# Routed experts of a gated Mamba/MoE layer: all tokens through all eight experts, against 40 sorted blocks of 256 chosen pairs

## The reference

```python
# branch s: Mamba block, 256 inner channels, 64 states
dt = softplus(x_ssm @ dt_w + dt_b)
state = state * exp(dt_t * A) + (dt_t * x_t)[:, :, None] * B_t[:, None, :]    # 512 steps, per channel and state
y_t   = einsum('bds,bs->bd', state, C_t)
s     = xn + ((y + x_ssm * D) * silu(z)) @ Wout
# branch g: 2 shared experts on every token, 8 routed experts of which the 2 best count
h_s    = experts(rmsnorm(xn), W1_s, b1_s, W2_s, b2_s).sum(experts)
scores = sigmoid(xn @ centroids)
gpk, i_topk = top_k(scores, 2);  gk = gpk / scores.sum(-1)
routed_all  = experts(rmsnorm(xn), W1_r, b1_r, W2_r, b2_r)        # 128 -> 512 -> gelu -> 128, dense in the reference
h_r    = (gk * take_along_axis(routed_all, i_topk)).sum(chosen)
g      = xn + h_s + h_r
```

## Time and profile before

| | us |
|---|---|
| median of 3 runs (lowest, highest) | 1951.54 (1948.29, 1955.75) |
| the profiled execution's own time | 1950.72 |
| its span, first to last instruction | 1949.0 |
| busy over the span: PE, DVE, ACT, POOL | 1700.5, 1851.6, 1344.5, 1333.7 |
| mean granted TensorE clock | 0.973 |

### The profile page before, as it was taken

One profiled execution on the slowest core, in us unless ns is written; L12 is line 12 of the kernel. 1 busy time (PEld: TensorE's weight loads), 2 busy tenths in 40 slices (PEclk: granted clock), 3 DMA queues, 4 the chain that ended last, 5 costly groups with the idle time before them and its releaser, 6 DMA issues.

```text
span 1949.0 us, 41413 instructions
## 1 busy us (share of the span) xinstructions
PE 1700.5 (87%) x10512; PEld 677.8 (35%) x10512; DVE 1851.6 (95%) x2100; ACT 1344.5 (69%) x2196; POOL 1333.7 (68%) x604
## 2 busy tenths in 40 slices
PE   1667579999999999999999999999999999999997
PEld 1433233333333333333333333333333333333332
DVE  6799669999999999999999999999999999999997
ACT  1478657777677777776777767777777677776773
POOL 6020057777777767776777777776777677777776
PEclk9689789999999999999999999999999999999999
DMA  4334455556555645564554745574566555465543
GB/s 126 119 111 148 148 152 118 116 117 153 123 116 121 163 118 122 120 146 130 118 117 116 162 121 115 122 161 119 122 119 148 133 120 115 117 161 120 116 116 93
DMA packets 191302, 248.49 MB, mean 127 GB/s; under 512 B 18714, under 2 KB 95140, under 8 KB 191084
## 3 DMA queue, kind: packets, MB, share of 16 engines
q1 hardware_dynamic: 191252, 247.76, 52.8%
HBM read 221.76 MB, written 25.30 MB: 127 GB/s over the span
## 4 chain that ended last, share of the span: by engine, by line
issue 32%; PE 27%; DVE 20%; POOL 10%; ACT 5%; SPq 2%; DVEq 2%; DMA 1%; ACTq 1%; POOLq 0%
DVE arena L910 10%; POOL arena L525 7%; DVE ps L900 6%; PE ps L1088 6%; PE ps L1074 6%; PE ps L1128 4%; PE ps L1120 4%; POOL arena L520 3%; ACT arena L676 1%; PE ps L1060 1%; PE ps L983 1%; PE ps L1134 1%; DMA gate_scratch<-arena 1%; SPq L250 1%; PE ps L1037 1%
## 5 line engine op out<-in xcount | busy, mean ns | idle before, releaser
L525 POOL TENSOR_TENSOR arena<-arena 128x1024 f32<-128x1024 f32 x512 | 1206.6, 2366 | 540.7 <-DVE arena L910 383.6
L910 DVE TENSOR_TENSOR_SCAN arena<-arena,ps 128x512 f32<-128x512 f32 x1024 | 1184.3, 1213 | 13.1 <-PE ps L1074 7.7
L676 ACT ACTIVATE arena<-arena,neg_A 128x512 f32 (+1 forms) x1024 | 657.9, 711 | 96.9 <-DVE arena L910 96.0
L1088 PE MATMUL ps<-arena,ident 64*64 64x512 f32 x4096 | 556.6, 615 | 3.2 <-POOL arena L525 3.2
L900 DVE TENSOR_TENSOR ps<-arena,ps 128x512 f32<-128x512 f32 x768 | 495.0, 697 | 17.9 <-PE ps L1060 16.9
L1120 PE MATMUL ps<-x_rms,arena 128*128 (+1 forms) x640 | 345.0, 637 | 74.6 <-ACT arena L698 72.1
L698 ACT ACTIVATE arena<-ps,b1r_sb 128x512 f32<-128x512 f32 x256 | 169.0, 686 | 270.8 <-PE ps L1120 270.0
L1074 PE MATMUL ps<-arena 128*64 128x128 f32 x4096 | 282.0, 280 | 23.5 <-DVE arena L910 18.1
L1074 PEld LDWEIGHTS ps<-arena 128*64 128x64 f32 x4096 | 220.5, 137 | 234.8 <-DVE arena L910 119.7
L1128 PE MATMUL ps<-arena 128*128 128x512 f32 x512 | 264.4, 618 | 0.0
L1120 PEld LDWEIGHTS ps<-x_rms,arena 128*128 128x128 f32 x640 | 101.6, 189 | 273.4 <-ACT arena L698 159.8
(11 more groups left out here) (122 smaller groups left out, 781.2 us busy)
## 6 DMA issues: line engine op xcount, KB each, us to landing
arena<-c_scratch SPq DMA_DIRECT2D x128, 1024.0 KB, 8.6
arena<-w_routed_scaled SPq DMA_DIRECT2D x128, 128.0 KB, 4.2
arena<-in_L_ffn_W_r_dram SPq DMA_DIRECT2D x64, 256.0 KB, 4.1
arena<-gate_scratch SPq DMA_DIRECT2D x64, 256.0 KB, 3.6
arena<-w_shared_tiles SPq DMA_DIRECT2D x128, 64.0 KB, 1.8
arena<-dt_scratch SPq DMA_DIRECT2D x9, 512.0 KB, 9.3
arena<-u_scratch SPq DMA_DIRECT2D x9, 512.0 KB, 10.2
arena<-xs_scratch SPq DMA_DIRECT2D x18, 256.0 KB
```

What stands on the lines that cost most here:

```text
L525: nc.gpsimd.tensor_tensor(products[:, i % RING, :, :], states[:, i % 2, :, :], c_rows[:, i // CG, i % CG, :].unsqueeze(1).broadcast_to((P, ...
L676: nc.scalar.activation(decay[:, 2 * i + h, :], dflat[:, ds(slot + h * L, L)], ACT.Exp, scale=aflat[:, ds(col, 1)]).then_inc(s["decay_ready ...
L910: vector.tensor_tensor_scan(states[:, i % 2, h, :], decay[:, m, :], ps[bank][:], 0.0, ALU.mult, ALU.add).then_inc(s["scanned"], 1)
L1088: ins = mm(y_ps[r][HP * h:HP * h + HP, :], ident[q, q], products[q, slot, h, :], start=False, stop=False, skip_group_check=True)
```

## The change

The routed experts no longer run on all tokens. In the preamble DVE picks the two best experts per token (`choose_experts`), PE counts by two matmuls how many pairs come before each token, and DVE gives each pair a row in a list sorted by expert, each expert rounded up to 256 rows (`place_tokens`). POOL scatters each token's normalised row to its two places by 64 indirect DMAs of 128 rows into a table that SP has filled with zeros. The sorted list has 40 blocks of 256 rows. Groups 0 to 39 (batches 0 to 4) take one block each, SP reading the block's expert from SBUF. Groups 40 to 63 take none. There POOL gathers the routed rows back by 64 indirect DMAs, three a group, and PE adds them, gated by diagonal matrices, into the final sum of each batch (`add_rows`). Per batch, the sums of both branches go through DRAM (`ffn_d`, `attn_d`), and the last steps of a batch (silu, product, turn, copy) come in three of the groups from 42 on. `KIND` becomes `DEDEDEDE`. W1 is scaled on ACT. `turns` is a Python list now, so that the preamble and the last three batches are written out and not looped.

```diff
-    KIND = "DDEDDDED"
+    KIND = "DEDEDEDE"
+    GATHERS = TOPK * TPB
+    GATHER_AT = (1, 4, 7)
...
+            sp.wait_ge(s["constants_made"], N_MASK)
+            sp.dma_start(x_sorted_d.rearrange("(n p) c -> p n c", p=P),
+                         zeros.unsqueeze(1).broadcast_to((P, NBLK * BK, C))).then_inc(s["zeros_stored"], 16)
...
-                load_w2(b, g)
-                load_gate(b, g)
-                load_w2_shared(b, g)
+                if block:
+                    load_w2(u, e)
+                if block_before:
+                    store_routed(u - 1)
+                load_w2_shared(u, g)
...
-            pool.wait_ge(s["w1_staged"], 32)
-            for g_col, a, n in ((g_routed_col, 0, E), (g_shared_col, E, ES)):
-                nc.gpsimd.tensor_scalar(w1_stage[:, a * H:(a + n) * H], w1_stage[:, a * H:(a + n) * H], g_col, None,
-                                        ALU.mult).then_inc(s["w1_scaled"], 1)
...
+            for j in range(NT):
+                for k in range(TOPK):
+                    nc.gpsimd.indirect_dma_start(x_sorted_d, bass.IndirectOffsetOnAxis(slots[:, k, j:j + 1], 0),
+                                                 rms_tok[:, j, :], None).then_inc(s["x_sorted"], 16)
+            pool.wait_ge(s["x_sorted"], 16 * TOPK * NT)
...
+            def gather(q):
...
+                nc.gpsimd.indirect_dma_start(rows[:, f % 2, at, :], None, routed_d,
+                                             bass.IndirectOffsetOnAxis(slots[:, k, f * TPB + j:f * TPB + j + 1], 0)
+                                             ).then_inc(s[f"rows_gathered{f % 2}"], 16)
...
+            def evict_block(m):
+                act.wait_ge(s["block_made"], m + 2)
+                act.wait_ge(s["routed_stored"], m * 16 + 16)
+                nc.scalar.copy(routed_out, block_ps[:, RA].rearrange("p (n c) -> p n c", c=C)
+                               ).then_inc(s["block_evicted"], 1)
...
+            def evict_attn(b):
+                act.wait_ge(s["attn_projected"], b + 2)
+                act.wait_ge(s["attn_stored"], b * 16 + 16)
+                nc.scalar.copy(attn_out, ffn_ps[:]).then_inc(s["attn_evicted"], 1)
...
+                    for t in range(HT):
+                        act.wait_ge(s["tile_made"], u * HT + (HT + t // 2 * 2 + 2))
+                        src = block_ps[:, (RA, RB)[t]] if t < 2 else hid_ps[:, (RA, RB)[t - 2]]
+                        nc.scalar.activation(hidden_block[:, t, :], src, ACT.Gelu, bias=b1_block[:, t:t + 1]
+                                             ).then_inc(s["tile_gelu"], 1)
...
+                    if i == 4 and block_before:
+                        evict_block(u - 1)
+                    if i == 6 and block:
+                        copy_x_block(u)
...
+                hidden_tiles(u, g, block)
+                if head and last is not None:
+                    evict_attn(last)
...
+                if k == 0:
+                    dve.wait_ge(s["w1_scaled_stored"], 32)
+                vector.tensor_tensor(rms_tok[:, j, :], xn_tok[:, j, :], bc3(stats[:, 7, j], C), ALU.mult
                                     ).then_inc(s["rms_made"], 1)
...
+            choose_experts()
+            for b, odd in turns:
                 convolve(b, b * NL + (base + NCONV - NL))
+                if b == 2:
+                    place_tokens()
...
-                    if i == SG - 2:
-
-                        dve.wait_ge(s["gate_row_loaded"], b * (16 * E) + g * 16 + 16)
-                        dve.wait_ge(s["expert_added"], b * E + g + 1)
-                        dve.wait_ge(s["expert_made"], b * E + g + 1)
-                        vector.tensor_tensor(gated_expert, expert_ps[:], gate_row, ALU.mult
-                                            ).then_inc(s["expert_gated"], 1)
+                    if last is not None and i == 2:
+                        gate_y(last)
...
+            def turn_x(m):
+                pe.wait_ge(s["x_rows_loaded"], m * 16 + 16)
+                pe.wait_ge(s["block_evicted"], m + 1)
+                for k in range(BK):
+                    ins = nc.tensor.transpose(block_ps[:, k * P:(k + 1) * P], x_rows[:, k, :], ident[:])
+                ins.then_inc(s["x_turned"], 1)
...
+                mm(bank[:, (RA, RB)[t % 2]], w1_block[:, t, :], x_block, start=True, stop=True, skip_group_check=True
+                   ).then_inc(s["tile_made"], 1)
...
+                for t in range(HT):
+                    ins = mm(block_ps[:, k * C:(k + 1) * C], hidden_block[:, t, k * P:(k + 1) * P], w2_block[:, t, :],
+                             start=(t == 0), stop=(t == HT - 1), skip_group_check=True)
...
-            W1_AT = {0: (2,), 1: (3,), 2: (4,)}
-            W1_NEXT_AT, W1_NEXT_BLOCK_AT = {7: (0, 1,)}, {7: (0, 1,)}
-            W2_AT = {2: (0,), 3: (1, 2,), 5: (3,), 7: (4,)}
+            TILES_AT = {0: (0, 1), 1: (2, 3)}
+            OUT_AT = {3: (0,), 4: (1,)}
+            NEXT_X_AT, SHARED_OUT_AT, NEXT_SHARED_AT = 6, 1, 7
```

More of the change, by code:

```diff
@@ new lines, in mamba_gated_moe @@
+        cur[0] = end - NE * L - 2 * NH * L
+        before, ones, zeros = take(P), take(P), take(C)
+        not_first_j = take(NT * E)
+        not_first_e = take(NT * E)
+        thresholds, block_no, ones_e = take(NTHR), take(NBLK), take(E)
+        over = take(E * NTHR, "p (e k) -> p e k", k=NTHR)
+        past = take(NBLK * E, "p (m e) -> p m e", e=E)
+        blocks, blocks_end, blocks_start = take(E), take(E), take(E)
+        slot_f = take(TOPK * NT, "p (k j) -> p k j", k=TOPK)
+        block_f = take(NBLK)
@@ new lines, in _ @@
+            load_open(0)
+            load_xn(0)
+            load_xn(1)
+            load_w1_shared(0, 0)
+            load_w2_shared(0, 0)
+            sp.wait_ge(s["slots_made"], 1)
+            e = expert_of(0)
+            load_w1_b1(0, e)
+            load_w2(0, e)
+            sp.wait_ge(s["x_sorted"], 16 * TOPK * NT)
+            load_x_rows(0)
+            load_batch(0, True)
+            with sp.Fori(1, NB_BLK) as b:
+                load_batch(b, True)
+            for b in range(NB_BLK, NB):
+                load_batch(b, False, b == NB_BLK)
@@ L627, in _ @@
                                 ).then_inc(s["scores_ready"], 1)
-            for b, odd in turns(act):
+            for b, odd in turns:
                 pad(b)
@@ L717, in _ @@
+            copy_u(0, 0, 0)
+            copy_u(0, 0, 1)
+            act.wait_ge(s["x_stored"], 16 * (NB + 1))
+            act.wait_ge(s["z_stored"], 16 * (NB + 1))
+            act.wait_ge(s["dt_u_made"], NB + 1)
+            run(0, True)
+            with act.Fori(1, NB_BLK) as b:
+                run(b, True)
+            for b in range(NB_BLK, NB):
+                run(b, False, b == NB_BLK)
+            silu_of(NB - 1, ffn_ps[:])
+            copy_result(NB - 1, hid_ps)
         @block.vector
@@ new lines, in group @@
+                    if next_block and i == (FIRST_NEXT_X_AT if first else NEXT_X_AT):
+                        turn_x(u + 1)
+                    if head and last is not None and i == PROJECT_AT:
+                        pe.wait_ge(s["ffn_evicted"], last + 1)
+                        project_out(last, 1 - odd, ffn_ps)
+                    if head and i == REOPEN_AT:
+                        if last is not None:
+                            pe.wait_ge(s["attn_evicted"], last + 1)
+                        open_ffn(b, odd)
```

728 lines of the change are left out of this document (452 added, 276 removed).

## The result

The changed kernel took 2006.39 us (median of four, 2002.95 to 2012.37), the kernel before beside it 1951.81. The ratio is 1.0282, with an interval of 1.025 to 1.0315: slower, where the prediction said 1859 and faster. The profiled execution has a span of 2003.4 us.

A forecast was written before the change was run, and what follows sets the result against it. DVE was taken to bind before, with PE 6% behind; after, PE binds block groups and DVE the rest. 1950.7 - 96 (main stage) + 0 (preamble) + 3 (end) = 1858, stated as 1859 us, range 1815 to 1935.

The forecast's parts named there:

- DVE bound before, relief finds PE: Steady stage before: DVE busy 394.1 of 400 us, PE 371.2, so a change relieving DVE soon meets PE.
- PE's block group 24.3: Groups with a block: PE's work sums to 24.2 us, above DVE's 22.56, so PE sets 24.3 (ends 23.4 and 25.8).
- PE dearer: Rival: bank wait binds or output matmuls cost 0.34; block groups 25.2 to 25.8, adding 35 to 58 us; chance 0.17.
- First groups of batches 1 to 4, +12: Each such group: 7.4 us extra PE work plus 4.5 with turn_x waiting behind evict_block and evict_attn; 12 a batch.
- X = 1.2 per indirect DMA on POOL: Each indirect DMA issue was taken to occupy POOL 1.2 us, half a product, between 0.35 and 7.5.
- POOL long: Rival: indirect DMAs hold POOL long, in last groups and scatter; chance 0.11 below the break, 0.10 slower beyond 2.4 us each.
- Groups 40 to 63 at 22.9: Groups without a block: PE 19.4 us with final sums beside it, DVE's 22.56 binds, POOL 22.6; 22.9 a group.
- Preamble about 0 (-12 to +15): Before the main stage: savings on DVE offset by zero-filling, the W1 store and 15 us of routing steps; net about 0.
- the 295: Sign of being wrong: group 1 starting later than 295 us.
- Hidden up to 1.9 a scatter: 64 preamble scatters on POOL from about 135 us cost nothing up to 1.9 us each; each 0.1 more costs 6.4.
- What would show it: Signs in busy time: last three batches DVE near 98%, PE near 85%; groups 1 to 39 PE nearly throughout, DVE about 93%.

The follow-up runs named there:

- e8: Changed kernel with final-sum loads issued a group early, each final sum one group later, and evict_attn moved behind evict_block: 1846.86 us, ratio 0.9442.
- e5: The changed kernel, unchanged, loaded again: 1958.72 us, ratio 1.0015 to the kernel before.
- e6: Changed kernel with the three loads of each final sum issued one group earlier, ahead of that group's other loads: 1929.82 us.
- e4: Changed kernel with each final sum one group later (ADD_IN is the gather group + 2): 1923.66 us.
- e7: Changed kernel with the final-sum loads issued one group earlier and each final sum one group later: 1896.39 us.
- e14: Changed kernel with only evict_attn moved on ACT behind evict_block, step 4 of a batch's second group: 1959.61 us, first scan at 280.5.
- e13: The changed kernel, unchanged, loaded once more: 2008.26 us, ratio 1.027 to the kernel before, first scan at 277.4.
- e16: The e8 version unchanged, loaded once more on another chip: 1897.89 us, first scan at 276.3.

## Why the prediction was wrong, point by point

The sum against the span, from the starts of scans (forecast: span 1856):

```
                              forecast   measured   difference
up to the first scan            235       275.0      +40
group 0                          45        47.3       +2
groups 1 to 39                  995.7    1002.8       +7
groups 40 to 63                 564.6     661.9      +97
end                                                   about 0
```

- **DVE bound before, relief finds PE.** Right. PE is busy 97% in block groups.
- **PE's block group 24.3** (sum 24.2). Measured 23.9; dense with four E steps 27.2 for 27.2. Prices by the distance of starts carry over to a new mix. The rival "PE dearer" (25.2 to 25.8) fell.
- **First groups of batches 1 to 4, +12.** The wait of `turn_x` is there, 4.52 for 4.5, at its place. But the second group is dear too (29.0 to 33.5 instead of 23.9): the term was 12 and is 14 to 18 over the two. 3.4 of the second group is PE's own work, as e8's 27.3 shows without the stop; the other 1.7 to 6.2 goes with the stop, and with it the clock's fall. A stop was priced by its length and not by what the clock loses around it. (In the kernel before, too, the second groups last 26.7 against 25.5; the prediction put it all in the first ones.)
- **X = 1.2 per indirect DMA on POOL.** 0.97 busy and 1.27 from one to the next while 64 follow each other, 0.99 and 1.01 between products; POOL was not held until the data land. The rival "POOL long" fell; its sign was right by another mechanism. The fit of the Trainium skill, "DMA: Bandwidth & Descriptors", section "Anatomy of one DMA — SWDGE (gpsimd) path", gives an estimate of 2.15 us for a whole transfer of 64 KB. The shortest here agree (2.2 for a scatter in e5), but the 64 gathers landed 2.5 to 10.5 us after their issue, 6.1 in the median, and the page's figure would be too short for them.
- **Groups 40 to 63 at 22.9, "the final sums fit beside it".** This is the step that failed, 97 of the 100 that are always there. The additions got no term: PE's surplus of 3 us (22.56 less 19.4) was taken to hold their work, and their waits were not looked for: three loads that SP issues 6 to 8 us before PE comes to them and that land after about 10, 27.4 in seven waits, and a gather issued at step 7 of the very group whose end needs it, 12.3 in two. e6 and e4 take 28 and 30 away, e7 58. `evict_attn` in a batch's first group takes 18 to 20 more (e7 to e8, e14). Of 97 e8 leaves 585.8 - 564.6 = 21. Part of that is PE's own work for an addition, which comes between two fills: 24.7 a group where one without it lasts 23.1. Only the last batch has groups at the 22.6 that was forecast.
- **Preamble about 0 (-12 to +15).** Without the hole the first scan is 9 us earlier than before (225.7 against 234.99), inside the bounds; the slots were ready at 118, not 135, and the scatter was hidden, as forecast. With the hole group 1 starts at 322, past the 295 that the prediction named as a sign of being wrong; without it, at 273.
- **"Hidden up to 1.9 a scatter."** Right for the data. But in two of four loadings of this program ACT stood for 57 to 59 us beside the scatter, and the start moved by 50; the prediction had no term for this. It had one for POOL alone. No row of before could show it, as that kernel has no software DMA, and what stops ACT is open.
- **What would show it.** DVE was not near 98% in the last three batches but 77 to 84%, PE not 85 but 83 to 85. That sign led to the step that failed.

The mechanism that the change rests on is sound: the block groups are 1.6 us shorter than before's 25.5, and with three repairs of order, none of which touches arithmetic, the kernel is at 1846.9 in a loading without the hole (1897.9 with it), where 1859 was forecast.

## What to carry to other kernels

An addition that "fits beside" the bound is three questions: its work, when its inputs are issued, and who stands behind it in order. Take each new instruction of the engine with slack, find the issue of its last input, and add a landing time of this kernel; a load issued 6 to 8 us ahead was late here, since it landed after about 10. A stop of TensorE can cost more than its length: look at the granted clock of the group behind it. Two halves of a change that move work in opposite directions between two engines have to be priced together: each alone was 3 to 6% slower here. And where a kernel begins to use a kind of DMA that it had not used, time more than one loading of it.

## What was not expected of the hardware

- Beside a burst of 64 indirect DMAs of GpSimd, ScalarE stood for 29 to 42 us at a stretch with nothing in the profile to release it and the DMA engines at 16% (first measurement and e13 to e16). It did so in 5 of 14 loadings with the full burst, on one chip in one loading and not in another. Waiting for the landing after every eight scatters cost 6 to 8 us, and the stop was not there in the two loadings that had the wait.
- In or at the end of a stop of TensorE of 4.5 us its granted clock fell, and the group behind it, in which TensorE was busy without a gap, took 29.0 to 33.5 us at a mean clock of 0.98 to 0.84, where it took 27.3 at 1.00 without the stop (the changed kernel, and e8 and e14). The same stop cost 1.7 us in one batch and 6.2 in another.
